# Deformable attention: sampling and similarities with the 16 small columns as the stationary side, on four column strips

## The reference

```python
# per window and group of 64 channels: B = 16 * 8 windows, G = 8 groups, 8 x 8 pixels
q = einsum('bgihw,goi->bgohw', xg, wq)
t = gelu(depthwise_conv(q, off_dw_w, stride 4) + off_dw_b)
off = tanh(einsum('bchw,oc->bohw', t, off_pw_w)) * 4.0          # 2 x 2 points per window and group
vgrid = ...                                                     # where the 4 points lie
kv = grid_sample(xg, vgrid)                                     # bilinear: 64 channels x 4 points
k = einsum('bgihw,goi->bgohw', kv, wk); v = einsum('bgihw,goi->bgohw', kv, wv)
sim = einsum('bhdi,bhdj->bhij', q * SCALE, k)                   # 64 pixels x 4 points per head
sim = sim + bias_mlp(qgrid - vgrid)
out = einsum('bhij,bhdj->bhdi', softmax(sim), v)
out = einsum('bchw,oc->bohw', out, w_out) + b_out
```

## Time and profile before

| | us |
|---|---|
| median of three runs | 3946.67 |
| profiled execution | 3954.3 |
| its span, first to last instruction | 3952.5 |
| TensorE matmul busy (share) | 3611.4 (91%) |
| VectorE busy | 2219.7 (56%) |
| ScalarE busy | 1585.3 (40%) |
| granted TensorE clock, mean | 0.961 |

### The profile page before, as it was taken

How to read it: one execution, slowest core, us unless ns; L and a number is a source line. 1 busy time by engine, 2 the same in 40 slices (tenths; PEclk the granted TensorE clock), 3 DMA queues, 4 the chain that set the end, 5 groups by cost and what they waited for, 6 DMA issues and landing times.

```text
span 3952.5 us, 47918 instructions
## 1 busy us (share of the span) xinstructions
PE 3611.4 (91%) x19232; PEld 2133.3 (54%) x19232; DVE 2219.7 (56%) x2875; ACT 1585.3 (40%) x2264; POOL 221.5 (6%) x165
## 2 busy tenths in 40 slices
PE   5989799899999999999999999999999899996988
PEld 2654457445664456644565445654457454573454
DVE  2554565466555565465654756537565475654755
ACT  0442443253433444253542635416343163432523
POOL 0000010001000020000200002000020000200200
PEclk9999999999999999899999999999999999998979
DMA  2011001300013000120011200121001300003020
GB/s 69 9 30 59 3 14 29 91 11 26 15 32 87 19 20 14 61 57 30 14 32 50 45 32 13 30 64 33 32 13 30 87 17 25 13 9 91 17 56 32
DMA packets 129422, 139.61 MB, mean 35 GB/s; under 512 B 78994, under 2 KB 98965, under 8 KB 128533
## 3 DMA queue, kind: packets, MB, share of 16 engines
q1 hardware_dynamic: 129204, 136.56, 12.5%
HBM read 99.48 MB, written 37.03 MB: 35 GB/s over the span
## 4 chain that ended last, share of the span: by engine, by line
PE 80%; DVE 7%; DMA 6%; ACT 4%; issue 3%; SPq 1%; POOL 0%; DVEq 0%; ACTq 0%; POOLq 0%
PE banks L472 14%; PE banks L507 12%; PE banks L522 10%; PE banks L491 10%; PE banks L535 7%; PE banks L653 4%; PE banks L552 3%; DMA x_dram<-exps 3%; PE banks L663 3%; PE banks L654 3%; PE banks L655 3%; PE banks L579 2%; PE banks L602 2%; PE banks L642 2%; DMA recips_dram<-recips 1%
## 5 line engine op out<-in xcount | busy, mean ns | idle before, releaser
L1053 DVE TENSOR_REDUCE neg_max<-banks 128x1 f32<-128x1024 f32 x512 | 602.6, 1218 | 415.7 <-PE banks L491 409.1
L828 ACT ACTIVATE exps<-banks,neg_max 128x1024 f32<-128x1024 f32 x512 | 565.0, 1112 | 209.9 <-DVE neg_max L1053 209.8
L838 ACT ACTIVATE exps_turned<-banks 128x1024 f32<-128x1024 f32 x256 | 262.2, 1024 | 927.5 <-PE banks L507 926.8
L507 PE MATMUL banks<-ident,exps 128*128 128x128 f32 x4096 | 570.3, 283 | 38.5 <-ACT exps_turned L838 19.3
L507 PEld LDWEIGHTS banks<-ident,exps 128*128 128x128 f32 x4096 | 449.3, 143 | 231.0 <-issue 231.0
L491 PE MATMUL banks<-qk_halves 64*128 64x512 f32 x3072 | 444.8, 422 | 87.0 <-ACT exps L828 43.1
L522 PE MATMUL banks<-exps_turned,values 128*64 128x256 f32 x4096 | 503.9, 389 | 15.3 <-DVE exps_turned L1062 8.5
L1062 DVE COPY exps_turned<-banks 128x1024 f32<-128x1024 f32 x256 | 313.1, 1223 | 239.5 <-PE banks L507 239.1
L491 PEld LDWEIGHTS banks<-qk_halves 64*128 64x128 f32 x3072 | 291.2, 193 | 282.6 <-issue 241.0
L1218 DVE SCALAR_TENSOR_TENSOR qk_halves<-banks,qk_halves 128x1024 fp32r<-128x1024 f32 x256 | 312.1, 1222 | 142.1 <-ACT qk_halves L867 140.5
L522 PEld LDWEIGHTS banks<-exps_turned,values 128*64 128x64 f32 x4096 | 278.5, 138 | 171.6 <-issue 64.2
(11 more groups left out here) (149 smaller groups left out, 3408.3 us busy)
## 6 DMA issues: line engine op xcount, KB each, us to landing
x_image<-in_x SPq DMA_DIRECT2D x8, 2048.0 KB, 8.8
recips_b<-recips_dram SPq DMA_DIRECT2D x256, 64.0 KB, 3.6
exps_turned<-in_x SPq DMA_DIRECT2D x32, 512.0 KB, 7.7
x_dram<-exps SPq DMA_DIRECT2D x32, 512.0 KB, 2.6
exps_turned<-x_dram SPq DMA_DIRECT2D x32, 512.0 KB, 20.0
out<-exps_turned SPq DMA_DIRECT2D x32, 512.0 KB, 2.7
attended<-mlp_rows SPq DMA_DIRECT2D x96, 112.0 KB
exps_turned<-in_wo SPq DMA_DIRECT2D x8, 1024.0 KB, 5.3
```

The source lines that it names most:

```text
L507: mm = pe.transpose(TB[:, kt // 4, kt % 4 * P:kt % 4 * P + P], PB[:, 2 * h + n % 2, kt * P:(kt + 1) * P], IDENT[:])
L828: freed(act.activation(PB[:, 2 * h + n % 2], slot(("s", m, i)), ACT.Exp, bias=NM[:, m:m + 1], accum_out=SS[:, m:m + 1]), ("s", m, i))
L1053: dve.tensor_reduce(NM[:, m:m + 1], slot(("s", m, i)), AX.X, ALU.max, negate=True).then_inc(mx, 1)
```

## The change

sample and similarities change sides. The small matrix becomes the stationary side, padded to 32 columns: WT gets 32 columns, of which 16 stay zero, and KZ is read 32 columns at a time from a flat tile KZR, of which the second 16 belong to the next block (their results are not used; 16 columns stand behind the last block). The 128 pixels or queries become the moving side. Tile t writes to the partitions 32t to 32t+31 of MB, its strip, and the four tiles of one block r stand next to each other in the program. As a strip is 128 columns wide for each r, MB holds four blocks, so each function runs in two halves f.

The result then has the small side on the partitions, so it is turned: ScalarE copies MB to the tile PW (keep_sampled, keep_similarities), TensorE transposes it in four pieces back to MB (turn_rows), and VectorE reads the wanted half of the columns (sampled, sim_rows, each in two halves).

```diff
+            def sample(f, j):
                 pe.wait_ge(wt_done, j + 1)
                 pe.wait_ge(xp_affine, j + 1)
-                for r in range(PXT):
+                wait_after(pe, kv_done, 2 * j + f)
+                for r in range(4):
                     for t in range(CT):
-                        c0 = (r * CT + t) * 16
-                        mm = pe.matmul(MB[:, c0:c0 + 16], XP[:, r, P * t:P * t + P], WT[:, r, t],
-                                       start=(c0 == 0), stop=True, skip_group_check=True)
-                mm.then_inc(kv_full, 1)
+                        mm = pe.matmul(MB[32 * t:32 * t + 32, P * r:P * r + P], WT[:, 4 * f + r, t],
+                                       XP[:, 4 * f + r, P * t:P * t + P], start=(r == 0), stop=True,
+                                       skip_group_check=True)
+                mm.then_inc(kvt_full, 1)
+
+            def turn_rows():
+                for r in range(4):
+                    mm = pe.transpose(MB[:, P * r:P * r + P], PW[:, P * r:P * r + P], IDENT[:])
+                return mm
+
+            def turn_sampled(f, j):
+                pe.wait_ge(kvt_done, 2 * j + f + 1)
+                turn_rows().then_inc(kv_full, 1)
...
+            def similarities(f, j):
+                pe.wait_ge(kz_done, j + 1)
+                wait_after(pe, sim_done, 2 * j + f)
+                for r in range(4):
+                    for t in range(CT):
+                        c0 = (t * WIN + 2 * (4 * f + r)) * 8
+                        mm = pe.matmul(MB[32 * t:32 * t + 32, P * r:P * r + P], KZR[:, c0:c0 + 32],
+                                       A[:, t, P * (4 * f + r):P * (4 * f + r) + P], start=(r == 0), stop=True,
+                                       skip_group_check=True)
+                mm.then_inc(simt_full, 1)
...
             def sampled_values(j):
-                pe.wait_ge(kz_done, j + 1)
+                pe.wait_ge(sim_done, 2 * j + 2)
+                if j + 2 < B:
+                    pe.wait_ge(gn_var, 2 * j + 4)
...
+            def keep_sampled(f, j):
+                act.wait_ge(kvt_full, 2 * j + f + 1)
+                act.activation(PW[:], MB, ACT.Copy).then_inc(kvt_done, 1)
...
                 for n in range(STEPS):
+                    if i and n in (25, 26):
+                        keep_sampled(n - 25, i - 1)
                     copy_turned(n, i)
                     if n + 1 < STEPS:
                         for h in range(2):
                             exp(n + 1, h, i)
+                    if i and n in (27, 28):
+                        keep_similarities(n - 27, i - 1)
...
-            def sampled(j):
-                dve.wait_ge(kv_full, j + 1)
+            def sampled(f, j):
+                dve.wait_ge(kv_full, 2 * j + f + 1)
                 for g in range(2):
-                    src = MB[64 * g:64 * g + 64].rearrange("p (b t u h e) -> p t b u h e", b=PXT, t=CT, u=2, h=2)
-                    dst = KV[64 * g:64 * g + 64].rearrange("p t (b u e) -> p t b u e", b=PXT, u=2)
+                    src = MB[64 * g:64 * g + 64].rearrange("p (b t z u h e) -> p z t b u h e", b=4, t=CT, z=2, u=2, h=2)[:, 0]
+                    dst = KV[64 * g:64 * g + 64].rearrange("p t (b u e) -> p t b u e", b=PXT, u=2)[:, :, 4 * f:4 * f + 4]
                     for w in range(2):
                         ins = dve.tensor_copy(dst[:, :, :, w], src[:, :, :, w, g])
```

More of the change, by code:

```diff
@@ L243, in build @@
         wt_done = sem("wt_done")
+        kvt_full = sem("kvt_full")
+        kvt_done = sem("kvt_done")
         kv_full = sem("kv_full")
@@ L595, in sampled_values @@
                 mm.then_inc(vp_full, 1)
[L597 to L605, removed]
             def pixels(i):
@@ L735, in _ @@
                         values(0, i + 1)
+                    if i and n == 25:
+                        turn_sampled(0, i - 1)
+                    if i and n == 26:
+                        turn_sampled(1, i - 1)
+                    if i and n == 27:
+                        similarities(0, i - 1)
+                    if i and n == 28:
+                        similarities(1, i - 1)
+                    if i + 1 < B and n == 29:
+                        wait_after(pe, sim_done, 2 * i)
+                        group_sums(2 * i + 2)
                     turn(n, 1, i)
@@ L743, in _ @@
                     if i and n == 24:
-                        sample(i - 1)
+                        sample(0, i - 1)
                     if i and n == 25:
+                        sample(1, i - 1)
+                    if i and n == 26:
                         sampled_keys(i - 1)
-                    if i and n == 26:
-                        sampled_values(i - 1)
[L749 to L754, removed]
+                    if i and n == 27:
+                        turn_similarities(0, i - 1)
+                    if i and n == 28:
+                        turn_similarities(1, i - 1)
+                    if i and n == 30:
+                        sampled_values(i - 1)
                 for half in range(2):
@@ L792, in _ @@
             turn_weights(B - 1)
-            sample(B - 1)
+            for f in range(2):
+                sample(f, B - 1)
+                turn_sampled(f, B - 1)
             sampled_keys(B - 1)
+            for f in range(2):
+                similarities(f, B - 1)
+                turn_similarities(f, B - 1)
             sampled_values(B - 1)
-            similarities(B - 1)
-            pe.wait_ge(sim_done, B)
+            pe.wait_ge(vz_done, B)
             mlp(B - 1)
@@ L962, in _ @@
             log(B - 1)
+            for f in range(2):
+                keep_sampled(f, B - 1)
+            for f in range(2):
+                keep_similarities(f, B - 1)
             mlp(B - 1, None)
@@ L971, in _ @@
         def _(dve):
-            for t in (WQB, WKB, WVB, PWZ, W3Z, WT, KZ, VZ, PW):
+            for t in (WQB, WKB, WVB, PWZ, W3Z, WT, KZR, VZ, PW):
                 dve.memset(t[:], 0.0)
@@ L1206, in value_blocks, with sim_rows @@
                 ins.then_inc(vz_done, 1)
-            def sim_rows(j):
-                dve.wait_ge(sim_full, j + 1)
+            def sim_rows(f, j):
+                dve.wait_ge(sim_full, 2 * j + f + 1)
                 for w in range(2):
                     rows = slice(64 * w, 64 * w + 64)
-                    ins = dve.tensor_copy(SM[rows], MB[rows].rearrange("p (n u e) -> p n u e", u=2, e=8)[:, :, w])
+                    ins = dve.tensor_copy(SM[rows, 16 * f:16 * f + 16],
+                                          MB[rows].rearrange("p (n z u e) -> p n z u e", z=2, u=2, e=8)[:, :, 0, w])
                 ins.then_inc(sim_done, 1)
@@ L1311, in _ @@
                     if i and n == 25:
-                        sampled(i - 1)
+                        sampled(0, i - 1)
                     if i and n == 26:
+                        sampled(1, i - 1)
+                    if i and n == 27:
                         key_blocks(i - 1)
-                    if i and n == 27:
+                    if i and n == 28:
+                        sim_rows(0, i - 1)
+                    if i and n == 29:
+                        sim_rows(1, i - 1)
+                    if i and n == 31:
                         value_blocks(i - 1)
-                    if i and n == 28:
-                        sim_rows(i - 1)
                     if i + 1 < B:
@@ L1339, in _ @@
                     copy_turned(n, i)
+                    if i + 1 < B and n == 29:
+                        group_variance(2 * i + 2)
                     if piece_of(n + 1) and n % 2 == 0:
@@ L1407, in _ @@
             weights_turned(B - 1)
-            sampled(B - 1)
+            sampled(0, B - 1)
+            sampled(1, B - 1)
             key_blocks(B - 1)
+            sim_rows(0, B - 1)
+            sim_rows(1, B - 1)
             value_blocks(B - 1)
-            sim_rows(B - 1)
             mlp(B - 1, None)
```

23 lines of the change are left out of this document (15 added, 8 removed).

## The result

The changed kernel takes 3861.16 us, the median of four runs (3860.42 to 3866.95); beside it the kernel before has a median of 3948.09. The ratio is 0.9779, 95% interval 0.9766 to 0.9792: 2.2% faster. The forecast was 3860, range 3836 to 3900. The profiled execution is the slowest of the four, 3866.95 with a span of 3865.0, so its times are a little long.

What follows compares the result with a forecast made beforehand. The prediction took TensorE to bound the kernel, with 80% of the chain that ended last. Gains of 63.0 - 3.6 + 17.0 - 0.4 + 11.0 = 87 us took 3954.3 to 3867, less 7.6 for the median: 3860, range 3836 to 3900.

Steps and rivals of the forecast that it cites:

- The price of a call: TensorE, sample and similarities: 0.95 us for each new call of 32 records, four strips side by side.
- rival of an issue bound: TensorE: short records cannot be issued at 29 ns, a call takes 1.86 us, total 3876 us; chance 0.16.
- rivals of strips one after another, at either clock: TensorE: strips do not overlap, 3.7 us a call, 3924, chance 0.08; with low clock 6.9, 4011, chance 0.03.
- What is late next: Step 25, mean of images 1 to 6: VectorE waits 5.9 us for the load of X, TensorE 6.2.
- the landing + 10.55: Images 1 to 6: scores(28) starts 10.55 us after the load of X lands, 23.3 after sample's start in the mean.
- The similarities: Steps 27 to 29: scores(31) comes 20.75 us after scores(28), at 44.0; gain 63 us over six images.
- 35.55 + 0.4: Image 7, which loads no X: scores(31) at 35.55 us from sample's start, plus 0.4 for sampled_values.
- The end: Image 7's sampling alone, after the images, at the low clock: 24.5 us instead of 35.5, gain 11.0.
- The sum: Whole kernel: 63.0 - 3.6 + 17.0 - 0.4 + 11.0 = 87 us gained.
- 3.6 for reciprocals: Step 29, six images: outputs waits for its reciprocals, 0.6 us each, 3.6 taken off the gain.
- rival of a clock that holds through the wait: TensorE's clock stays high through the wait for X, 16 us less in up to six images: 3844; chance 0.11.

Runs made afterwards that it cites:

- e5: Changed kernel with the two loops of sample and similarities exchanged, so the strips follow each other: 3866.19 us, ratio 0.9799 to the kernel before.
- e1: Changed kernel with the load of the next image's X issued on SyncE ahead of recips_around(11): 3792.32 us, ratio 0.9625 to the kernel before.
- e6: Changed kernel with the early load of X, plus the loops of sample and similarities exchanged: 3834.49 us, ratio 0.9726 to the kernel before.
- e3: Changed kernel with similarities and sim_rows as before, so only sampling is changed: 3911.24 us, ratio 0.9925 to the kernel before.
- e4: Changed kernel with sample and sampled as before, so only similarities are changed: 3869.03 us, ratio 0.9818 to the kernel before.

## Why the prediction was right

**The price of a call.** Forecast 0.95 as pitch (from its start to the next instruction's), measured 1.01. It came from two rows: mlp3 showed that four strips overlap, a plain transposing what one record of 128 moving columns costs. The trace has it so: the four records of a set start within 0.02 us, and the sets 0.11 apart. The rival of an issue bound (1.86) is refuted by 32 records in 1.08; its extra of 0.96 a call should have read 0.91, which moves its 3876 by less than 1 us. The rivals of strips one after another, at either clock, are refuted by the same rows, and e5 shows that not even strips in turn take 3.7. The Trainium skill's floor of some 25 ns between starts ("TensorE: Matmul & The Clock Gate", Part 1, Wait — 56ns, not 53.3ns?) agrees with the mean over a call, 32 ns a record, but not with the single starts in a set, which lie 7 ns apart. Its 62 ns, which it gives for matmuls decoded in software, does not apply here: a call would take 2.0 us by it.

Not in the sum: what TensorE loses where it changes to strips or back. Ahead of sample(0) the transposing took 1.02 us to the next start, and 0.93 ahead of the old full-width sample; behind the last record of similarities the transposes start 0.20 us later, and 0.11 is the distance of full-width records. That is 0.09 at a change that can be read by itself; the one into similarities can't, as a wait lies in it. At 0.09 eight changes would make 0.7 us in an image and 5 in all, an estimate. The drain at a change of mode of which the Trainium skill speaks ("TensorEngine Tiling (Array Packing)", Key Properties) would have to fit in these 0.09; the forecast priced it at up to about 10 in all and left it out.

**What is late next.** Forecast: VectorE waits 5.9 us for the load in the mean of six images; measured 5.8. TensorE 6.2, measured 6.0 in the mean and 7.26 in image 2. scores(28) at the landing + 10.55: measured 10.6 behind it in the mean of six, and at 23.3 where 23.3 was forecast; in image 2 it is 25.1 for 24.5. The landing itself came right by two small errors against each other: the load was issued 3.65 us after the start of sample in the mean, for 3.94, and took 9.0 us, for 8.8. e1, e5 and e6 show that it is this wait, and e3 and e4 that the sampling half is worth so little for it.

**The similarities.** 20.75 from scores(28) to scores(31) forecast, 20.6 to 21.3 measured; the mean scores(31) of the six at 44.0 in both. There was no low clock around similarities, as forecast. outputs in step 29 waited for its reciprocals 0.31, 0.93, 0.24 and 1.23 us in images 2 to 5 and not in 1 and 6, 0.45 in the mean; the forecast took 0.6. Not forecast: in image 2 VectorE waits 1.35 us in step 28 before copy_turned, and turn(29,0) of TensorE waits 0.63 behind it. turn(28,1) had ended 1.28 us before that copy began. In image 4 the copy began 0.93 late in the same way, in the other five images 0.04 to 0.19; what held it is not shown. Image 7 took 36.3 for 35.55 + 0.4. sampled_values took the place of a wait, as forecast: behind it 0.39 us of idle time are left of the 1.41 of the earlier trace rows.

**The end.** 24.5 forecast, 24.0 measured; a call at the low clock 1.95 and 1.93, the copy 0.60 in both.

**The sum.** 87 us forecast. The profiled execution is 87.4 shorter than that of before (3954.3 to 3866.95), and the medians differ by 86.9. That it is so close is partly luck. In the stretches that the forecast priced, the two traces differ by 91: six images gave 63.2, where the forecast had 63.0 less 3.6 for reciprocals, image 7 gave 16.3 for 16.6, the end 11.5 for 11.0. The 3.6 was the one term clearly too careful, since the images came out at 44.0 with these waits inside. Against that the rest of the execution took 3.5 more: ahead of the first sample the changed kernel needed 3.8 us more, of which 1.1 is image 0's longer wait for X and the rest is not explained, and between scores(31) and the next sample single images took up to 1.7 us more or 2.4 less. The profiled run of the changed kernel is also 6 us above its fastest.

The rival of a clock that holds through the wait was wrong: the granted clock fell to its lower level in all six images before TensorE went on, in image 3 (wait 5.2 us) for 3.4 us, in the others for 6.8 or 10.2.

## What to carry to other kernels

When an engine's long call gets short, ask of every transfer that ends inside it when it is issued and what its issue waits for: here the load stood in SyncE's order behind a round trip that had nothing to do with it, and that place cost 61 us once its cover was gone, about 9 before. In this kernel it paid to put a small operand on the stationary side of neighbouring strips, with neighbours in the program on different strips: two calls of 1.08 us in place of one of 8.6 to 11.5, even with the copy and the turn that it needs. A stretch of the old trace that lacks the work you are about to shorten (image 0, without sampling) was the best model of what the stall would look like.

## What the runs showed of the hardware that was not expected

Records on one strip followed by those of the next still overlap in part: 32 records took 2.46 us with the strips in turn, and 1.08 with the strips alternating; one after another they would take 3.7, an estimate from 0.116 a record. With the strips in turn the next strip starts with the fifth of the eight records of the strip before. And a 2 MB load ahead of the 2 KB store of the reciprocals did not make that round trip longer: in image 2 of e1_early_load the store was issued at 1068.48 and the loads behind it at 1078.01, 9.5 us later, where the changed kernel needed 10.9. In the mean of the six images it is 8.1 us for 9.5.
